# Three pairs of PSUM banks in place of two for the radial products of a graph convolution, and its sums in banks 6 and 7

## The reference

```python
R = jax.nn.relu(abs_distances[:, None] @ w1 + b1) @ w2 + b2     # radial weights, one row per edge
Y = spherical_harmonics(rel_vec)
Fj = features[src]                                              # a gather, one row per edge
...
acc = acc + _NORM[i] * jnp.einsum('euv,ef,evi,ofi->euo', Rb[..., k], Yf, Fb, C)
...
out = out.at[dst].add(msg)                                      # scatter-add to the nodes
```

## Time and profile before

| | us |
|---|---|
| median of 3 runs | 11822.15 (11821.74 to 11833.75) |
| profiled execution, its own time | 11825.35 |
| its span | 11823.7 |
| main part of the convolution, from DVE's first product to the last group's end | about 8036 to 11558 |
| the three turns of the rest | about 11558 to 11823 |

### The profile page before, as it was taken

How to read it: one execution, slowest core, us unless ns; L and a number is a source line. 1 busy time by engine, 2 the same in 40 slices (tenths; PEclk the granted TensorE clock), 3 DMA queues, 4 the chain that set the end, 5 groups by cost and what they waited for, 6 DMA issues and landing times.

```text
span 11823.7 us, 340699 instructions
## 1 busy us (share of the span) xinstructions
PE 7408.7 (63%) x130038; PEld 4971.8 (42%) x130039; DVE 9354.8 (79%) x19079; ACT 3124.7 (26%) x7571; POOL 5296.6 (45%) x5027
## 2 busy tenths in 40 slices
PE   2555555200877877777777787775666666666663
PEld 2444444100766666666666676661222222222221
DVE  8777777457777877777777777778999999999995
ACT  0111111057222222222222222223333333333331
POOL 3777777400321221231131122116667766676773
PEclk9999999965988988888898898885555555555555
DMA  4111111067745754654564575551111111111111
GB/s 168 26 25 26 26 25 26 27 233 272 205 146 148 208 150 150 177 166 148 163 189 148 161 208 162 160 151 37 34 32 33 32 31 34 32 33 32 31 32 19
DMA packets 718056, 1212.33 MB, mean 103 GB/s; under 512 B 186449, under 2 KB 334068, under 8 KB 713636
## 3 DMA queue, kind: packets, MB, share of 16 engines
q1 hardware_dynamic: 434084, 1058.42, 28.6%
q0 software_dynamic: 146832, 69.31, 5.7%
q10 hardware_dynamic: 136012, 67.95, 2.4%
HBM read 1050.89 MB, written 140.94 MB: 101 GB/s over the span
## 4 chain that ended last, share of the span: by engine, by line
PE 37%; DVE 18%; issue 18%; DMA 4%; POOL 3%; DVEq 1%; ACT 1%; SPq 0%; POOLq 0%; ACTq 0%
PE psum L1814 9%; PE psum L1782 9%; PE psum L1901 7%; PE psum L1797 6%; DVE space L1383 2%; DVE space L1351 2%; PE psum L1898 2%; DMA space<-src_rows 2%; POOL space L772 2%; PE psum L1859 2%; DVE space L1387 1%; PE psum L1886 1%; DVE space L1394 1%; DMA space<-slots 1%; PE psum L1870 1%
## 5 line engine op out<-in xcount | busy, mean ns | idle before, releaser
L772 POOL DMA_INDIRECT space<-feature_table,space x2000 | 2430.5, 1215 | 598.3 <-issue 587.9
L700 POOL TENSOR_TENSOR claim_out<-claim_in 128x1 f32<-128x1 f32 x443 | 108.3, 245 | 5072.1 <-DMA table<-space 2639.0
L1901 PE MATMUL psum<-w_mix,space 64*128 64x448 f32 x4144 | 1818.2, 974 | 0.0
L1532 ACT ACTIVATE space<-psum 128x375 f32<-128x375 f32 x2400 | 955.1, 436 | 3006.7 <-PE psum L1782 2963.9
L709 POOL DMA_INDIRECT slots<-space x1568 | 1506.7, 961 | 466.1 <-issue 412.8
L1137 DVE TENSOR_TENSOR space<-psum,space 128x320 f32<-128x320 f32 x2400 | 1069.0, 486 | 786.1 <-PE psum L1797 715.6
L1782 PE MATMUL psum<-space 128*32 128x125 fp8e4 x72000 | 1341.1, 224 | 255.8 <-issue 253.2
L1814 PE MATMUL psum<-space 128*128 128x96 bf16 x24000 | 1292.6, 207 | 235.4 <-issue 146.2
L1782 PEld LDWEIGHTS psum<-space 128*32 128x32 bf16 x72000 | 1079.2, 98 | 509.8 <-issue 504.5
L1814 PEld LDWEIGHTS psum<-space 128*128 128x128 fp8e4 x24000 | 1105.3, 97 | 391.3 <-issue 270.9
L755 POOL DMA_INDIRECT space<-table,space x864 | 1099.4, 1272 | 280.9 <-issue 280.9
(11 more groups left out here) (289 smaller groups left out, 11803.5 us busy)
## 6 DMA issues: line engine op xcount, KB each, us to landing
space<-marks SPq DMA_DIRECT2D x2400, 320.0 KB
space<-src_rows SPq DMA_DIRECT2D x102, 640.0 KB, 4.7
marks<-space SPq DMA_DIRECT2D x100, 640.0 KB, 3.2
space<-distances ACTq DMA_DIRECT2D x200, 320.0 KB, 4.8
space<-block_ids SPq DMA_DIRECT2D x198, 200.0 KB
slots<-space SPq DMA_DIRECT2D x83, 448.0 KB, 9.1
space<-feature_table,space POOLq DMA_INDIRECT x2072, 2.7
slots<-space POOLq DMA_INDIRECT x1608, 2.1
```

The costliest lines, as they stand in the source:

```text
L772: g.indirect_dma_start(out=gathered_rows[0:SLOTS, half, t, :], out_offset=None, in_=feature_table, in_offset=bass.IndirectOffsetOnAxis(ap= ...
L1532: a.activation(to[:, s0:s1, :, :], pair_picked[:, bank, 0:(s1 - s0) * PICK_COLS].rearrange("p (k c r) -> p k c r", k=s1 - s0, r=CAP), ACT.Copy
L1901: last = mm(radial[:, 2 * pair + odd, 0:MIX_S + MIX_V], hidden[odd * HIDDEN:(odd + 1) * HIDDEN, slot, pair * LANES:(pair + 1) * LANES], w2 ...
```

## The change

`radial` gets banks 0 to 5, three pairs of banks, and `conv_sums` moves to banks 6 and 7. In the main part the pairs go round these three in the order in which they are used, counted within a turn of 20 pairs (`TURN_PAIRS`). PE's sequence for group n becomes: pair 3 of group n, pairs 0, 1 and 2 of group n+1, `add_group(n)`. A pair waits until the one three places before it has been used; the first two of a turn wait until the one two places before has been used (20 is no multiple of 3, so the ring starts anew). The rest (`Over`) keeps two pairs of banks and its order. Its transposed distances lie in bank 7, which now also holds `conv_sums`, and so PE waits once for the last `move_sums` ahead of that loop.

```diff
+    TURN_PAIRS = PAIR_GROUPS * GROUP_PAIRS
+    RADIAL_PAIRS = 3
...
-        radial, conv_sums, half_sums = banks(0, QUAD), banks(4, 2), banks(4, 4)
+        radial, conv_sums, half_sums = banks(0, 2 * RADIAL_PAIRS), banks(6, 2), banks(4, 4)
...
+                def ring_of(g, pair):
+                    return (g * GROUP_PAIRS + pair) % RADIAL_PAIRS
...
+                def ring_of(g, pair):
+                    return pair % 2
...
-                at, bank = slice(2 * pair, 2 * pair + 2), slice(2 * (pair % 2), 2 * (pair % 2) + 2)
+                at, ring = slice(2 * pair, 2 * pair + 2), kind.ring_of(g, pair)
+                bank = slice(2 * ring, 2 * ring + 2)
...
-            def radial_pair(nth, slot, pair):
-                pe.wait_ge(hidden_ready, nth + 1)
-                pe.wait_ge(radial_used, 2 * nth + pair + 1)
+            def radial_pair(group, pair, ring, held):
+                slot, upper = divmod(pair, 2)
+                pe.wait_ge(hidden_ready, 2 * group + slot + 1)
+                pe.wait_ge(radial_used, GROUP_PAIRS * group + pair + 3 - held)
...
+            def main_pair(group, g, pair):
+                at = (g * GROUP_PAIRS + pair) % TURN_PAIRS
+                radial_pair(group, pair, at % RADIAL_PAIRS, 2 if at < 2 else RADIAL_PAIRS)
...
-            first_quad(0)
+            for pair in range(3):
+                main_pair(0, 0, pair)
...
-                        second_quad(nth)
-                        first_quad(nth + 1)
+                        main_pair(nth, g, 3)
+                        for pair in range(3):
+                            main_pair(nth + 1, g + 1, pair)
                         add_group(nth, g)
...
+            pe.wait_ge(sums_moved, CHUNKS + 1)
             with pe.Fori(0, turns, 1) as i:
```

More of the change, by code:

```diff
@@ L1892, in _, with over_pair @@
             pe.wait_ge(weights_spread, 16 * 3)
-            def radial_pair(nth, slot, pair):
-                pe.wait_ge(hidden_ready, nth + 1)
-                pe.wait_ge(radial_used, 2 * nth + pair + 1)
+            def radial_pair(group, pair, ring, held):
+                slot, upper = divmod(pair, 2)
+                pe.wait_ge(hidden_ready, 2 * group + slot + 1)
+                pe.wait_ge(radial_used, GROUP_PAIRS * group + pair + 3 - held)
                 for odd in range(2):
-                    mm(radial[:, 2 * pair + odd, 0:MIX_S + MIX_V], ones_bf[odd * HIDDEN:odd * HIDDEN + PARTS, :],
+                    mm(radial[:, 2 * ring + odd, 0:MIX_S + MIX_V], ones_bf[odd * HIDDEN:odd * HIDDEN + PARTS, :],
                        bias_bf[odd * HIDDEN:odd * HIDDEN + PARTS, :], start=True, stop=False)
                 for odd in range(2):
-                    last = mm(radial[:, 2 * pair + odd, 0:MIX_S + MIX_V],
-                              hidden[odd * HIDDEN:(odd + 1) * HIDDEN, slot, pair * LANES:(pair + 1) * LANES],
+                    last = mm(radial[:, 2 * ring + odd, 0:MIX_S + MIX_V],
+                              hidden[odd * HIDDEN:(odd + 1) * HIDDEN, slot, upper * LANES:(upper + 1) * LANES],
                               w2_mix[odd * HIDDEN:(odd + 1) * HIDDEN, :], start=False, stop=True)
                 last.then_inc(radial_ready, 1)
[L1906 to L1912, removed]
+            def main_pair(group, g, pair):
+                at = (g * GROUP_PAIRS + pair) % TURN_PAIRS
+                radial_pair(group, pair, at % RADIAL_PAIRS, 2 if at < 2 else RADIAL_PAIRS)
+            def over_pair(group, pair):
+                radial_pair(group, pair, pair % 2, 2)
             def add_group(nth, g):
@@ L1944, in _ @@
                 for g in range(PAIR_GROUPS):
-                    second_quad(m * PAIR_GROUPS + g)
-                    first_quad(m * PAIR_GROUPS + g + 1)
-                    add_group(m * PAIR_GROUPS + g, g)
+                    nth = m * PAIR_GROUPS + g
+                    main_pair(nth, g, 3)
+                    for pair in range(3):
+                        main_pair(nth + 1, g + 1, pair)
+                    add_group(nth, g)
             for g in range(PAIR_GROUPS):
                 nth = (UNIT_PAIRS - 1) * PAIR_GROUPS + g
-                second_quad(nth)
+                main_pair(nth, g, 3)
                 if g + 1 < PAIR_GROUPS:
-                    first_quad(nth + 1)
+                    for pair in range(3):
+                        main_pair(nth + 1, g + 1, pair)
                 add_group(nth, g)
@@ L1973, in _ @@
                                     ).then_inc(spill_turned_ready, 1)
-                first_quad(i * SPILL_GROUPS + MAIN_GROUPS)
+                for pair in range(2):
+                    over_pair(i * SPILL_GROUPS + MAIN_GROUPS, pair)
                 for g in range(SPILL_GROUPS):
                     nth = i * SPILL_GROUPS + g + MAIN_GROUPS
-                    second_quad(nth)
+                    for pair in range(2, GROUP_PAIRS):
+                        over_pair(nth, pair)
                     if g + 1 < SPILL_GROUPS:
-                        first_quad(nth + 1)
+                        for pair in range(2):
+                            over_pair(nth + 1, pair)
                     add_over(nth, g)
```

## The result

The changed kernel takes 11671.07 us (median of 4 runs, 11652.5 to 11694.34) beside 11827.95 for the kernel before (median of 4); the ratio is 0.9863, 95% interval 0.9835 to 0.9890. The forecast was 11618 in a range of 11590 to 11690.

A forecast was written before the change was run, and what follows sets the result against it. DVE was taken as the bound, with its waits for PE removable: 261.2 regained, less 58.8 lost to late gathers, plus 2.3, less 0.5, gives 204 us; 11822 - 204 = 11618 us, range 11590 to 11690.

The forecast's parts named there:

- The waits for PE: DVE's waits at L1347 ahead of m2 and m3: 446 waits, 225.5 us of idle time, all predicted to go.
- the 1.06 us in hand: Pair 3 readable at s + 3.60, m3 wanting it at s + 4.66, so m3 would not wait for PE.
- The overlap: In front of m2 and m3, each removed wait gives about 0.08 us beyond its idle time, 261.2 us in all.
- the sum: Main part and rest: 261.2 - 58.8 + 2.3 - 0.5 = 204 us saved.
- The way to group 0's rows: From L1394 of g = 2 through reload and gathers to L1320 in g = 4: stays 17.64 us, losing 58.8 us.
- "slower" rival: POOL becomes the bound as busier DVE holds up gathers at L772; at 1.80 us a gather, 11917 us; chance 0.04.
- Group 1's rows: Rows land at D + 30.70, g = 0 projects at D + 30.78; cost 0 to 15 us, taken as 0.
- a changed way and a second wait in g = 0: Signs of a wrong forecast: the D to L1320 time changes, or DVE waits again for rows in g = 0.
- Idle only: Rival at m2 and m3: the overlap does not come back, 176 us saved, 11646 us; chance 0.11.
- No gather bound: Rival: the way from D to L1320 is shorter, g = 3 keeps its gain, 11559 us; chance 0.06.
- The wait only moves: Rival: pair 3 carries the whole delay, m3 waits what m2 and m3 did, about 11820 us; chance 0.05.
- A second late transfer: Rival: group 1's rows land 1 us later, losing 49 us, 11667 us; chance 0.10 shared with a late m3.

The follow-up runs named there:

- the kernel with the early signal: Changed kernel with the signal for the reload moved ahead of L1403, behind L1396, carried by a one-column memset; main part 3281.5 us, ratio 0.9805 to the kernel before.
- the banks-only kernel: Kernel before with only the convolution's sums moved to banks 6 and 7 and PE's added wait ahead of the rest; main part 3526.3 us, ratio 0.9997.

## Why the prediction was right, step by step

**The waits for PE: right.** 446 waits, 225.5 us, are all gone; the last group's 2.6 became 0.4. Pair 3 starts 1.20 us into the group, and m3 never waits ahead of that last group, as the 1.06 us in hand had said.

**The overlap: right, and the rule set against it was quoted in half.** From L1328 to m2 the changed kernel has 0.81 us (9516.87 to 9517.68), from L1338 to m3 0.66 (9532.29 to 9532.95), the two distances of the earlier trace rows. The three instructions at L1328 last to 9517.77, and the next one starts at 9517.68. Over the whole main part the distances in front of m2 and m3 became 263.9 us shorter, where the sum had 261.2 and the idle time alone is 225.5: the 0.08 a wait came back. The prediction had set the Trainium skill's page VectorE: DVE Perf Modes, section "The DRAIN you can't avoid", against them: no start before the pipeline is empty. The same paragraph of the Trainium skill goes on: "A next op that is not held starts earlier". The prediction left that out. So the page, read whole, doesn't exclude the overlap that the trace shows.

**The way to group 0's rows: right in kind, 0.3 us short in size.** It stayed, as said, while everything round it became shorter, and the wait at its end is now the largest of DVE's: 102.7 us in 49 waits, 2.1 each, where the prediction had 1.8. The step that failed is "No part of this is PE's or DVE's, so it stays 17.64". The mean was 17.6 before and 17.9 after, with all of the difference in the eight gathers, 12.0 and then 12.3 us, and their length does depend on DVE. Of the main part's 2000 gathers 246 last over 1.25 us after, and 180 before, and every one of them starts inside a DVE product with both inputs in SBUF, or within 0.1 us ahead of it. Before, the seventh and the eighth gather of the way were such ones, 1.32 and 1.38 us on average; after, it is the sixth and the seventh, 1.57 and 1.40. DVE's changed phase has put the sixth near the start of the longest of these products (1.7 us in 32 of 49 turns), where the seventh had at most started late in it. 49 x 0.3 = 15 us. That the product holds the gather is shown by the kernel whose L1396 reads PSUM.

This also answers what the prediction said beside the Trainium skill's page SBUF — State Buffer, section "The single rule": "No row here shows a gather held up by one." One did, the 1.31 us gather at 10066.78 in the earlier trace rows; it starts 0.19 us behind L1401, a product with both inputs in SBUF. The held gathers fit the shared ports that the page of the Trainium skill names. Its inference under the same rule, that a `tensor_tensor` doesn't hold up the making of a DMA's descriptors, doesn't fit them (1.67 us and not 1.20), and the measurement decides. Nor does all of the lock show here. A lock held for a whole instruction would also make the product wait behind a gather, but in the kernel with the early signal L1396 starts at 10205.19, inside the gather of 10204.73, and takes its 0.76 us. The "slower" rival was given 0.04, and its point of 1.75 us a gather wasn't near: gathers take 1.226 us on average, before 1.215.

**Group 1's rows: on the wrong side of a bound.** "That just holds" had 0.1 us in hand, cost 0 to 15, taken at 0. It did not hold: 37 short waits, 13.3 us of idle time, and 16.7 from start to start, since these waits take the overlap away again. The value taken was the wrong end of its bound of 15, and the truth lay a little over it. The gathers' 0.3 us can't be the cause, for DVE starts g = 0 that much later too. The rows land later behind their gather. POOL's sixteenth gather of the half and SP's reload of the second half, in the turn of the earlier trace rows:

```profile
10079.07 1.26 POOL L772 DMA_INDIRECT space<-feature_table,space  x1 [0.31 <-issue]
10080.34 0.26 SPq L655 DMA_DIRECT2D space<-slots  x1
```

and after, with ACT's copy that shows when the rows land:

```profile
9526.12 1.21 POOL L774 DMA_INDIRECT space<-feature_table,space  x1 [0.31 <-issue]
9526.92 0.26 SPq L657 DMA_DIRECT2D space<-slots  x1
9530.43 0.26 ACT L1614 ACTIVATE space<-space 128x64 f32<-128x64 f32 x1 [6.20 <-DMA space<-feature_table,space]
```

DVE's earlier end of g = 4 lets SP reload earlier. By the trace's DMA records (medians of 49 turns) the reload's first packet starts 1.7 us behind the start of this gather, before 2.2, and the gather's last packet ends 3.6 us behind it, before 2.7. In the kernel whose L1396 reads PSUM, where the way is only 17.4, it is 3.6 too, and there are 40 short waits. This is the prediction's rival of a landing that moves by about 1 us with the changed phase. That the reload holds up the rows is argued from the times alone; no run moved it by itself. The prediction had named a changed way and a second wait in g = 0 as signs of being wrong. Both came, and both were small.

**The sum, then.** 204.7 us for the main part, less 14.9 and 16.7 for these two steps, are 173.1; measured are 179.8. The sum lacked 6.7 on the other side. Of these, 2.7 are the distances in front of m2 and m3 (263.9 and not 261.2). Another 4.1 lie right behind these products: one that has waited lasts some 0.01 us longer than one that has not (0.69 and 0.68 us in the rows), and there were 446 of them. That they offset part of the two mis-sized steps is luck.

**The time ahead of the convolution.** The medians differ by 156.9 us (11827.95 and 11671.07), 47 less than the sum of 204. The shorter saving in the main part accounts for 25 of these, and the rest behind it gave 1 back. The convolution of the changed kernel began 14.9 us later in its profiled run, and the profiled runs differ by 165.4. Some 8 more lie between profiled run and median, where single runs of the changed kernel range over 42 us. With the banks-only kernel, whose code ahead of the convolution does the same work as that of before, the convolution began 11.7 later. So a difference of that size needs no cause in the change, though the one repeat that could have settled it ran on another chip, and it stays open.

**The rivals.** Idle only would have made the main part about 177 us shorter, close to what was measured, but for a reason that the distances exclude: the overlap came back (263.9 and not 225.5), and the gathers took nearly as much away. By the total alone the two could not be told apart. No gather bound: out, by the kernel with one gather more. The wait only moves: out, no wait for PE is left. A second late transfer: came, with a landing 0.9 us later, at about a third of the 49 us that it was priced at (16.7), since in most turns these rows had landed well before they were wanted. Slower: out, as said.

## What to carry to other kernels

When a wait in a loop goes away, look for the longest path that leaves the engine and comes back in the same loop (signal, reload, gathers, use), and ask which part of the loop's gain lies within it: that part is not gained. Lengthening this path by a known amount is the sharpest test of whether it binds, here 1.5 us a turn and 74 us in all. And once a buffer has been added so that work is ready earlier, the consumer's own order can be set anew: doing m2 before the projection, and giving the signal at the last reader, gave another 99 us for a few moved lines.

## What the runs showed of the hardware

A gather issued by POOL takes 1.20 us, but 1.67 us when it starts 0.15 us behind the start of a DVE product of 0.76 us with both inputs in SBUF, and 1.38 us when it starts 0.45 us behind it (9510.69). It takes 1.39 us when it starts 0.1 us behind the start of such a product of 0.42 us (9512.38). With one of the two inputs in PSUM it takes 1.20 us at the same place. Where the product starts 0.46 us behind the gather (10204.73 and 10205.19 in the kernel with the early signal) the gather takes 1.20, so it is held only at its beginning, and the product is not held by it. None of the 1373 gathers of the changed kernel's main part that start away from such products lasts over 1.25 us. In the changed kernel this comes to 1.226 us for the mean gather, and it costs time because two such starts in each turn lie on the path that sets the turn.
